# Loads issued part by part, array work ahead of the first norm, value copies on ScalarE, and a new order between two batches of a post-norm transformer block

## The chip, the cores and the metric

The kernel runs on one core of one Trainium2 chip, in one launch. The metric is the device time in microseconds (us). The kernel before took 471.42 us as the median of 3 runs (471.38 to 472.26).

## The reference

For two sequences of 1024 tokens of width 256, in fp32:

```
Xn  = layernorm(X) * ln_g + ln_b
Q, K, V = Xn @ Wq + bq, Xn @ Wk + bk, Xn @ Wv + bv        # 16 heads of 16
A   = softmax(causal(Q K^T / 4));  attn = (A V) @ Wo + bo
x   = layernorm(X + attn)
h   = relu(x @ W1 + b1);  alpha = softmax(h @ W2 + b2)     # 8 maps
y   = layernorm(x + sum_k alpha_k * (x @ V_k^T) @ U_k^T)
```

The rows of A sum to one, so bv can be added to the output of the attention, as `bv @ Wo`, in place of being added to every value.

## The kernel before, in words

Tokens are cut into 8 tiles of 128, and two chunks c of 512; heads into four groups g of four. A list of events, written out in `program_order` (L143 to L213), is walked by every engine; each issues the instructions that it has for an event, in that order, with waits on semaphores between the engines. `attention_order` weaves row maxima, scores and value products of one batch, and `beside` (L183 to L192) hangs further events on its steps; the steps run to 47, so an event at 48 to 50 stands at the end of the batch's attention.

The events that matter here:

- `ln1` (L608), `ln2` (L690), `ln3` (L724): the three norms, on VectorE, four tiles at a time; each is a chain of small instructions.
- `xt` (L762): the normed input is transposed by PE into a bank of PSUM and copied by ScalarE (L517) to `xt`, which lies in the probabilities' buffer `pr[2]`.
- `qk` (L776): PE computes a part of Q or K (m is the half of the heads, w is 0 for Q and 1 for K); ScalarE writes its bf16 high part (L531, semaphore `s_high`), VectorE the rest (L626); `part` then makes the middle part on ScalarE (L536, `s_mid`) and the low part on POOL (L489, `s_low`). The exact fp32 product of a score is rebuilt from six bf16 products.
- `stack` (L420): twelve DMAs, issued by SP, that copy the parts of four heads to the stacks `stq` and `stk`, in two halves of two heads; six of them fill one half.
- `v` (L782): PE computes the values of two tiles in a bank, VectorE adds bv and writes them to `va` (L632). There are four of these in a batch.
- `max` (L790, L646): PE recomputes scores, VectorE takes the row maximum; `split` and `rows` turn the maxima into three rows that are sent to `stq` by DMA; `score` (L812) and `value` (L824) are the attention proper, with the exponentials on ScalarE (L545).
- `ot`, `r1`: the attention's output is transposed and multiplied by Wo; `bo` (L478, POOL) has added bo to the input. `x1t`, `h`, `lg`, `weigh`, `alpha`: the gates. `vx`, `avt`, `u`: the maps.

PSUM is used as two rings. Results for VectorE go to four banks in turn (`n_dve`), those for ScalarE to three (`n_act`); PE may take a bank only when the result that had it before has been read:

```
        n_act = count("xt", "score", "ot", "x1t", "h", "avt")
        n_dve = count("qk", "v", "max", "rows", "turn", "r1", "lg", "vx", "u")
```

SP's queue holds, in the order of the events, the loads of X, of the weights, the stacks, the rows and the stores. Between the batches (b = 0 to 1) the order is

```
            order += ot + first[:parts] + [r4, r6, n] + first[parts:parts + 2] + m[0][9:]
            order += [("load", nb)] + turned + first[parts + 2:parts + 3] + mixed[:parts] + first[parts + 3:]
            order += [("stack", nb, 1, 0)] + mixed[parts:] + second[:parts] + [("alpha", b, 1)] + third[b][:1]
```

where `first` and `second` are xt, qk and stack of the next batch's chunks 0 and 1, `[r4, r6, n]` the last r1 pair and ln2 of this batch, `turned` x1t, `mixed` h, lg and weigh, `m[0][9:]` the last two u, and `third` ln3.

Of the kernel before, what the change touches and what calls it, by code (L numbers as in the profile page):

```python
# [12 lines left out]
P = 128  # L13
# [129 lines left out]
def program_order(batches, groups, tiles, parts):  # L143
# [34 lines left out]
    for b in range(batches):  # L178
# [6 lines left out]
        if nb < batches:  # L185
            beside[30] = [("early", nb)]
            beside[38] = [("ln1", nb, 0, TPC)]
            beside[43] += [("ln1", nb, TPC, TPC)]
        for k, t in zip((13, 17, 21, 25), pairs):
            beside[k] = [("bo", b, t)]  # L190
# [13 lines left out]
        if nb < batches:  # L204
            first, second = begin(nb, 0), begin(nb, 1)
            before = m[1]
            order += ot + first[:parts] + [r4, r6, n] + first[parts:parts + 2] + m[0][9:]
            order += [("load", nb)] + turned + first[parts + 2:parts + 3] + mixed[:parts] + first[parts + 3:]
            order += [("stack", nb, 1, 0)] + mixed[parts:] + second[:parts] + [("alpha", b, 1)] + third[b][:1]
# [6 lines left out]
def block_kernel(nc, x, vecs, rows, wq, wk, wv, wo, w1, w2, vt, ut, out):  # L216
# [16 lines left out]
    with ExitStack() as ctx:  # L233
# [15 lines left out]
        flat = sb("flat", [P, 2 * D + E])  # L249
        ident = sb("ident", [P, P])  # L250
# [48 lines left out]
        s_flat = sem("s_flat")  # L299
        s_w = {n: sem(f"s_w_{n}") for n in ("qk", "v", "o", "1", "2", "vt", "ut")}  # L300
# [33 lines left out]
        n_act = count("xt", "score", "ot", "x1t", "h", "avt")  # L334
        n_dve = count("qk", "v", "max", "rows", "turn", "r1", "lg", "vx", "u")
# [57 lines left out]
        def _(sp):  # L393
# [3 lines left out]
            for ev in order:  # L397
                kind, b = ev[:2]
                if kind == "load":
# [9 lines left out]
                    if b == 0:  # L409
                        sp.dma_start(flat[:], rows.partition_broadcast(P)).then_inc(s_flat, 16)  # L410
                        weight(w_v[:], wv, "v")
                if kind == "early":
# [7 lines left out]
                if kind == "stack":  # L420
                    _, _, g, c = ev

                    sp.wait_ge(s_low, n_part["part", b, KC - 1, c, 1])
# [5 lines left out]
                    for i in range(2):  # L429
# [4 lines left out]
                        row = 0  # L434
                        for part_of_q, parts_of_k in ((0, 3), (1, 2), (2, 1)):
                            rows_ = slice(row, row + parts_of_k * DH)
                            row = rows_.stop
                            same = q_parts[:, part_of_q:part_of_q + 1].to_broadcast([DH, parts_of_k, KC * CHUNK])
                            sp.dma_start(k[rows_, c, heads], k_parts[:, 0:parts_of_k]).then_inc(s_stack[stack_of(b, g)][c][i], 16)
                            sp.dma_start(q[rows_, c, heads], same).then_inc(s_stack[stack_of(b, g)][c][i], 16)  # L440
# [19 lines left out]
        def _(pool):  # L460
# [15 lines left out]
            for ev in order:  # L476
                kind, b = ev[:2]
                if kind == "bo":  # L478
                    pool.wait_ge(s_flat, 16)
# [250 lines left out]
        def _(pe):  # L730
# [29 lines left out]
            for ev in order:  # L760
# [63 lines left out]
                if kind == "value":  # L824
# [8 lines left out]
                    if g == 0:  # L833

                        pe.wait_ge(s_dve_free, n_dve["v", b, kt // 2 * 2])
# [98 lines left out]
```

## Time and profile before

| | |
|---|---|
| median of 3 runs | 471.42 us |
| the profiled execution, its own time | 473.8 us |
| span of the profile | 472.1 us |
| PE busy | 416.1 us, 88% |
| PE weight loads | 208.1 us, 44% |
| VectorE busy | 314.9 us, 67% |
| ScalarE busy | 230.4 us, 49% |
| POOL busy | 73.4 us, 16% |
| mean granted TensorE clock | 0.966 |

The page gives the busy time of each engine over the whole span. The timeline gives instructions in order of time, neighbours of one kind merged: "x16" on a row is a run of 16 of them, and its second number the time from the first's start to the last's end.
### The profile page before, as it was taken

To read this page: it belongs to the slowest core of one execution; us is meant where nothing else is said; L and a number is where in the kernel's file an instruction comes from. 1 tells how busy PE (TensorE), PEld (TensorE's weight loads), DVE (VectorE), ACT (ScalarE), POOL (GpSimd) and SP (SyncE) were. 2 spreads that over 40 slices of the span, in tenths; PEclk is the share of its full clock that TensorE was granted. 3 is DMA by queue.
4 is the path that set the end of the run, shared out by engine and by line. 5 is a ranking of instruction groups with operands and counts; after the bars stand their busy time and mean duration, and the time that the engine had idled before them with its cause. 6 is when DMAs were issued, how large, how long until landed. Compare 5 with 4: busy or idle time off the path is not lost.

```text
span 472.1 us, 7166 instructions
## 1 busy us (share of the span) xinstructions
PE 416.1 (88%) x2512; PEld 208.1 (44%) x2512; DVE 314.9 (67%) x812; ACT 230.4 (49%) x490; POOL 73.4 (16%) x108
## 2 busy tenths in 40 slices
PE   1798897998999989997899989799899999997893
PEld 1355343343344433475447734334334443356452
DVE  5448895898798676244557799689889771225266
ACT  6451554666668475332441155476666846431210
POOL 2042121033120101101120021113222020110000
PEclk9999897999999999998899999899999999999997
DMA  5048883370502000002287028146050000000011
GB/s 179 0 53 101 181 100 41 43 94 3 68 24 69 2 1 0 1 0 91 29 103 115 1 62 104 17 61 77 12 59 3 0 2 0 2 0 0 1 45 44
DMA packets 18147, 21.13 MB, mean 45 GB/s; under 512 B 4672, under 2 KB 11584, under 8 KB 18112
## 3 DMA queue, kind: packets, MB, share of 16 engines
q1 hardware_dynamic: 18061, 20.66, 27.8%
q8 instruction: 20, 0.33, 0.3%
q14 instruction: 15, 0.12, 0.1%
q10 hardware_dynamic: 51, 0.01, 0.0%
HBM read 5.78 MB, written 2.10 MB: 17 GB/s over the span
## 4 chain that ended last, share of the span: by engine, by line
PE 64%; DVE 21%; ACT 6%; DMA 3%; issue 3%; SPq 2%; POOL 0%; DVEq 0%; ACTq 0%
PE ps L756 24%; PE ps L841 13%; PE ps L821 12%; DVE mx L646 11%; PE ps L800 9%; ACT pr L545 2%; DMA stq<-mrow 2%; PE ps L804 2%; PE ps L750 2%; ACT stk L508 2%; DVE st L595 1%; DVE x L602 1%; PE ps L851 1%; PE ps L886 1%; DMA cols<-in_vecs 1%
## 5 line engine op out<-in xcount | busy, mean ns | idle before, releaser
L545 ACT ACTIVATE pr<-ps 128x512 f32<-128x512 f32 (+3 forms) x384 | 167.7, 495 | 129.6 <-PE ps L821 127.9
L646 DVE TENSOR_REDUCE mx<-ps 128x1 f32<-128x512 f32 (+3 forms) x304 | 182.1, 654 | 31.4 <-PE ps L804 23.3
L821 PE MATMUL ps<-stq,stk 99*128 99x512 bf16 (+3 forms) x384 | 119.0, 338 | 13.6 <-DMA stq<-mrow 8.0
L800 PE MATMUL ps<-stk,stq 96*128 96x512 bf16 (+3 forms) x384 | 115.8, 333 | 3.9 <-DVE mx L646 1.4
L498 POOL TENSOR_SCALAR_AFFINE_SELECT pr<-pr 128x512 f32<-128x512 f32 x64 | 40.8, 637 | 274.2 <-ACT pr L545 274.2
L841 PE MATMUL ps<-pr,va 128*32 128x512 f32 (+3 forms) x768 | 82.3, 501 | 0.0
L821 PEld LDWEIGHTS ps<-stq,stk 99*128 99x128 bf16 x384 | 35.1, 99 | 101.0 <-ACT pr L545 53.2
L804 PE MATMUL ps<-mask,ident_b 128*128 128x128 bf16 x256 | 50.3, 223 | 0.0
L800 PEld LDWEIGHTS ps<-stk,stq 96*128 96x128 bf16 x384 | 38.0, 99 | 24.4 <-issue 8.3
L756 PE MATMUL ps<-pr,w_qk 128*128 128x512 f32 x64 | 34.8, 697 | 4.2 <-ACT pr L517 4.2
L756 PE MATMUL ps<-u_t,avt 128*128 128x256 f32 x128 | 30.9, 387 | 2.8 <-ACT avt L567 2.8
L756 PE MATMUL ps<-v_t,x_t 128*128 128x512 f32 x64 | 32.1, 629 | 0.0
L804 PEld LDWEIGHTS ps<-mask,ident_b 128*128 128x128 bf16 x256 | 25.6, 100 | 12.8 <-issue 4.2
L489 POOL TENSOR_TENSOR qk_raw<-res,qk_raw 128x512 bf16<-128x512 f32 x16 | 18.3, 1157 | 70.1 <-ACT qk_raw L536 70.1
L626 DVE SCALAR_TENSOR_TENSOR res<-ps,cols,qk_raw 128x512 f32<-128x512 f32 x16 | 11.9, 750 | 24.7 <-ACT qk_raw L531 20.9
L841 PEld LDWEIGHTS ps<-pr,va 128*32 128x32 f32 x768 | 15.3, 108 | 29.3 <-issue 20.2
L715 DVE TENSOR_TENSOR avx<-ps,alpha 128x512 f32<-128x512 f32 x16 | 11.0, 690 | 23.0 <-PE ps L756 23.0
L756 PEld LDWEIGHTS ps<-u_t,avt 128*128 128x128 f32 x128 | 23.4, 191 | 6.0 <-DVE x L723 3.2
L531 ACT ACTIVATE qk_raw<-ps,cols 128x512 bf16<-128x512 f32 x16 | 11.0, 687 | 29.6 <-PE ps L756 29.6
L756 PEld LDWEIGHTS ps<-pr,w_qk 128*128 128x128 f32 x64 | 14.1, 227 | 21.3 <-issue 20.6
L567 ACT ACTIVATE avt<-ps 128x512 f32<-128x512 f32 x16 | 9.5, 597 | 27.3 <-PE ps L886 27.3
L756 PEld LDWEIGHTS ps<-v_t,x_t 128*128 128x128 f32 x64 | 11.9, 199 | 10.6 <-issue 9.5
(75 smaller groups left out, 338.8 us busy)
## 6 DMA issues: line engine op xcount, KB each, us to landing
stk<-qk_raw SPq DMA_DIRECT2D x32, 96.0 KB, 2.8
stq<-qk_raw SPq DMA_DIRECT2D x32, 96.0 KB, 3.1
x_in<-in_x SPq DMA_DIRECT2D x8, 256.0 KB, 3.3
stk<-qk_raw SPq DMA_DIRECT2D x32, 64.0 KB, 3.2
stq<-qk_raw SPq DMA_DIRECT2D x32, 64.0 KB, 3.2
out_y<-x SPq DMA_DIRECT2D x3, 512.0 KB, 3.0
stk<-qk_raw SPq DMA_DIRECT2D x32, 32.0 KB, 2.9
stq<-qk_raw SPq DMA_DIRECT2D x32, 32.0 KB, 2.5
```

The lines of the kernel that those rows point to most:

```text
L489: pool.tensor_tensor(part(w, c, 2)[:, m], res[:, n_part[ev] % RES], part(w, c, 1)[:, m], ALU.subtract).then_inc(s_low, 1)
L498: pool.affine_select(out=blk, in_=blk, compare_op=ALU.is_ge, fill=0.0, base=0, pattern=[[0, HPG], [1, P]], channel_multiplier=-1).then_inc ...
L531: nc.scalar.activation(part(w, c, 0)[:, m], dve_bank(ev), ACT.Identity, bias=cols[:, 2 + w, m:m + 1]).then_inc(s_high, 1)
L545: nc.scalar.activation(probs(b, g, s)[:, j, q0 - c * CHUNK:], act_bank(ev)[:, q0 - c * CHUNK:], ACT.Exp, scale=DH ** -0.5).then_inc(s_act_ ...
L626: nc.vector.scalar_tensor_tensor(res[:, n_high[ev] % RES], dve_bank(ev), cols[:, 2 + w, m:m + 1], part(w, c, 0)[:, m], ALU.add, ALU.subtra ...
L646: nc.vector.tensor_reduce(dst, src, AX.X, ALU.max).then_inc(s_dve_free, 1)
L715: nc.vector.tensor_tensor(avx[:, t % 2, :].rearrange("p (e r) -> p e r", e=E), dve_bank(ev).rearrange("p (e r) -> p e r", e=E), alpha[:, t ...
L756: last = nc.tensor.matmul(out_, lhs(k), rhs(k), start=(k == 0), stop=(k == n - 1))
L800: last = nc.tensor.matmul(bank[:, i * w:(i + 1) * w], q[0:ROWS, t // TPC, j, tile(t % TPC)], k[0:ROWS, k0 // CHUNK, j, 0:w], start=True, s ...
L804: last = nc.tensor.matmul(bank[:, (i + 1) * w - P:(i + 1) * w], ident_b[:], mask[:], start=False, stop=True)
L821: nc.tensor.matmul(bank[:, q0 - c * CHUNK:], stk[stack_of(b, g)][0:ROWS + PARTS, kt // TPC, j, tile(kt % TPC)], stq[stack_of(b, g)][0:ROWS ...
L841: last = nc.tensor.matmul(values_bank[j * VW:(j + 1) * VW, q0 - c * CHUNK:], va[:, kt, g * HPG + j, :], probs(b, g, s)[:, j, q0 - c * CHUNK:],
```

## The change

The order changes, both in what hangs on the attention's steps and between the batches. A new event `fold` in the first batch computes `bv @ Wo` on PE, with bv as a stationary operand that is repeated over 128 columns, and VectorE adds it to the row of bo that `bo` later adds to the input. The values are then copied from PSUM by ScalarE without a bias, and take a bank of ScalarE's ring. A stack's DMAs wait for the part that they copy, the high parts first, and the pairs are regrouped so that each pair needs one further part. PE runs 20 matmuls of a constant by itself before its first transposes and 5 behind those of the first chunk (`turn_over`); their result is overwritten.

```diff
@@ program_order
+            beside[49] = m[0][7:8] + [("xt", nb, 0, k) for k in ks]
             beside[43] += [("ln1", nb, TPC, TPC)]
+        if b == 0:
+            beside[9] = [("fold", 0)]
...
-            order += ot + first[:parts] + [r4, r6, n] + first[parts:parts + 2] + m[0][9:]
-            order += [("load", nb)] + turned + first[parts + 2:parts + 3] + mixed[:parts] + first[parts + 3:]
-            order += [("stack", nb, 1, 0)] + mixed[parts:] + second[:parts] + [("alpha", b, 1)] + third[b][:1]
+            qk, (here, xt, later) = first[parts:-1], (first[-1:], second[:parts], [("stack", nb, 1, 0)])
+            order += qk[:1] + ot + qk[1:2] + m[0][9:10] + [r4, r6, n] + m[0][10:] + qk[2:3] + [("load", nb)]
+            order += turned + qk[3:] + here + later + third[b][:1] + xt + mixed + [("alpha", b, 1)]
@@ counts
-        n_act = count("xt", "score", "ot", "x1t", "h", "avt")
-        n_dve = count("qk", "v", "max", "rows", "turn", "r1", "lg", "vx", "u")
+        n_act = count("xt", "v", "score", "ot", "x1t", "h", "avt")
+        n_dve = count("qk", "fold", "max", "rows", "turn", "r1", "lg", "vx", "u")
@@ SP, load
                         weight(w_v[:], wv, "v")
+                        for k in range(KC):
+                            sp.dma_start(bv[:, k:k + 1], rows[k * P:(k + 1) * P].rearrange("(p o) -> p o", o=1)).then_inc(s_bv, 16)
@@ SP, stack
-                    sp.wait_ge(s_low, n_part["part", b, KC - 1, c, 1])
...
-                        for part_of_q, parts_of_k in ((0, 3), (1, 2), (2, 1)):
...
+                        made = ((s_high, n_high["qk", b, KC - 1, c, 1]), (s_mid, n_part["part", b, KC - 1, c, 1]),
+                                (s_low, n_part["part", b, KC - 1, c, 1]))
+                        for part_of_q, row, terms in ((0, 0, 3), (1, 3 * DH, 2), (2, 5 * DH, 1)):
+                            sp.wait_ge(*made[part_of_q])
+                            q_rows, k_row = slice(row, row + terms * DH), (5 * DH, 3 * DH, 0)[part_of_q]
+                            k_rows = slice(k_row, k_row + (part_of_q + 1) * DH)
+                            same = q_parts[:, part_of_q:part_of_q + 1].to_broadcast([DH, terms, KC * CHUNK])
+                            sp.dma_start(q[q_rows, c, heads], same).then_inc(s_stack[stack_of(b, g)][c][i], 16)
+                            sp.dma_start(k[k_rows, c, heads], k_parts[:, 0:part_of_q + 1]).then_inc(s_stack[stack_of(b, g)][c][i], 16)
@@ POOL, bo
-                    pool.wait_ge(s_flat, 16)
+                    pool.wait_ge(s_dve_free, n_dve["fold", 0])
@@ ScalarE
+                if kind == "v":
+                    t = ev[2]
+                    act.wait_ge(s_act_full, n_act[ev])
+                    nc.scalar.activation(va[:, t:t + 2, :, 0:DH], act_bank(ev).rearrange("p (t h d) -> p t h d", t=2, h=HEADS),
+                                         ACT.Copy).then_inc(s_act_free, 1)
@@ VectorE (the add of bv in "v" goes)
+                if kind == "fold":
+                    dve.wait_ge(s_flat, 16)
+                    dve.wait_ge(s_dve_full, n_dve[ev])
+                    nc.vector.tensor_tensor(flat[:, D:2 * D], dve_bank(ev)[:, 0:D], flat[:, D:2 * D], ALU.add).then_inc(s_dve_free, 1)
@@ PE
+            def turn_over(n):
+                for _ in range(n):
+                    nc.tensor.matmul(values_bank, ident_b[:], ident_b[:].unsqueeze(1).to_broadcast([P, TPC, P]),
+                                     start=True, stop=True)
+
+            pe.wait_ge(s_mask, 4)
+            turn_over(20)
             pe.wait_ge(s_ident, 2)
...
                     turn(bank, src, k).then_inc(s_act_full, 1)
+                    if ev == ("xt", 0, 0, KC - 1):
+                        turn_over(5)
...
+                if kind == "fold":
+                    bank = take_dve(ev)
+                    weights("o", b)
+                    pe.wait_ge(s_bv, 16 * KC)
+                    product(bank[:, 0:D], lambda k: bv[:, k:k + 1].to_broadcast([P, P]), lambda k: w_o[:, k, :], KC).then_inc(s_dve_full, 1)
                 if kind == "v":
-                    bank = take_dve(ev)
+                    bank = take_act(ev)
...
-                        pe.wait_ge(s_dve_free, n_dve["v", b, kt // 2 * 2])
+                        pe.wait_ge(s_act_free, n_act["v", b, kt // 2 * 2])
```

## Rows read from the trace of the kernel before

**Rows 1.** The page: the chain that ended last, shares of the span by engine.

```profile
PE 64%; DVE 21%; ACT 6%; DMA 3%; issue 3%; SPq 2%; POOL 0%; DVEq 0%; ACTq 0%
```

**Rows 2.** Timeline, first 46 us, PE: start us, us, instruction, [idle before, releaser].

```profile
14.64 9.66 PE L756 MATMUL ps<-pr,w_qk 128*128 128x512 f32 x16 [2.55 <-ACT pr L517]
25.01 3.62 PE L756 MATMUL ps<-w_v,pr 128*128 128x256 f32 x16
28.47 7.03 PE L756 MATMUL ps<-pr,w_qk 128*128 128x512 f32 x16
...
44.96 0.24 PE L810 MATMUL ps<-ident_b,mhl 128*48 128x128 bf16 x1 [0.50 <-DMA stq<-qk_raw]
45.40 0.22 PE L800 MATMUL ps<-stk,stq 96*128 96x128 bf16 x1 [0.20 <-issue]
```

**Rows 3.** Timeline, PE, two bf16 matmuls of 512 columns.

```profile
78.09 1.06 PE L821 MATMUL ps<-stq,stk 99*128 99x512 bf16 x2
```

**Rows 4.** Timeline, first 46 us, ScalarE and VectorE.

```profile
5.72 7.29 ACT L508 ACTIVATE stk<-minus 3x2048 f32<-3x2048 f32 x4
13.04 1.45 ACT L517 ACTIVATE pr<-ps,cols 128x512 f32<-128x512 f32 x2
...
24.34 0.69 ACT L531 ACTIVATE qk_raw<-ps,cols 128x512 bf16<-128x512 f32 x1 [0.51 <-PE ps L756]
...
26.38 1.43 ACT L517 ACTIVATE pr<-ps,cols 128x512 f32<-128x512 f32 x2
...
36.92 3.40 DVE L646 TENSOR_REDUCE mx<-ps 128x2 f32<-128x512 f32 x6
40.66 0.69 DVE L632 TENSOR_TENSOR va<-ps,flat 128x512 f32<-128x512 f32 x1 [0.33 <-PE ps L756]
41.27 2.81 DVE L646 TENSOR_REDUCE mx<-ps 128x2 f32<-128x512 f32 x5
...
44.83 0.68 DVE L632 TENSOR_TENSOR va<-ps,flat 128x512 f32<-128x512 f32 x1
```

**Rows 5.** Timeline, SP's queue: the loads of the first two stacks (24 in all).

```profile
27.93 0.72 SPq L439 DMA_DIRECT2D stk<-qk_raw  x1
...
43.13 0.59 SPq L440 DMA_DIRECT2D stq<-qk_raw  x1
```

**Rows 6.** Timeline between the batches, PE.

```profile
211.73 1.89 PE L756 MATMUL ps<-u_t,avt 128*128 128x256 f32 x8
216.43 2.45 PE L756 MATMUL ps<-u_t,avt 128*128 128x256 f32 x8 [2.81 <-ACT avt L567]
...
232.10 8.44 PE L756 MATMUL ps<-pr,w_qk 128*128 128x512 f32 x12 [1.67 <-ACT pr L517]
240.38 1.88 PE L756 MATMUL ps<-v_t,x_t 128*128 128x512 f32 x4
```

**Rows 7.** Stretches: us, busy time (and count) by engine, then clock, DMA share, GB/s.

```profile
217.90:221.20 3.30, 3.30 (x12) 2.54 (x11) 0.42 (x1) 1.17 (x2) 0.25 (x1) 0.50 0.38 118
...
231.30:238.10 6.80, 6.00 (x7) 2.50 (x8) 5.96 (x26) 1.34 (x2) 0.12 (x1) 0.51 0.70 83
...
240.40:271.10 30.70, 30.70 (x160) 21.57 (x158) 21.38 (x57) 5.75 (x10) 4.32 (x4) 1.00 0.49 70
```

**Rows 8.** Timeline between the batches, VectorE.

```profile
208.85 1.41 DVE L595 BATCH_NORM_STATS2 st<-x_in 128x6 f32<-128x256 f32 x4
...
213.09 1.38 DVE L602 TENSOR_SCALAR x<-x_in,mv,rstd 128x256 f32<-128x256 f32 x4
...
271.38 1.88 DVE L632 TENSOR_TENSOR va<-ps,flat 128x512 f32<-128x512 f32 x3
```

**Rows 9.** Two more stretches, with the columns of rows 7.

```profile
446.20:449.60 3.40, 3.40 (x6) 1.46 (x5) 1.25 (x4) 0.06 (x1) 0.00 (x0) 0.54 0.01 2
...
76.40:79.50 3.10, 3.09 (x10) 1.25 (x10) 1.12 (x2) 1.93 (x4) 0.00 (x0) 0.50 0.02 5
```

**Rows 10.** Groups by form: count | busy us, mean ns | idle before, releaser.

```profile
L756 PE MATMUL ps<-w_o,o_t 128*128 128x256 f32 x64 | 15.1, 383 | 0.8 <-ACT o_t L522 0.8
```

More of the change, by code:

```diff
@@ L249, in block_kernel @@
         flat = sb("flat", [P, 2 * D + E])
+        bv = sb("bv", [P, KC])
         ident = sb("ident", [P, P])
@@ L299, in block_kernel @@
         s_flat = sem("s_flat")
+        s_bv = sem("s_bv")
         s_w = {n: sem(f"s_w_{n}") for n in ("qk", "v", "o", "1", "2", "vt", "ut")}
@@ L433, in _ @@
                         k_parts = parts(1, c)[head].rearrange("p n m s -> p n (m s)")
-                        row = 0
-                        for part_of_q, parts_of_k in ((0, 3), (1, 2), (2, 1)):
[L436 to L440, printed above, removed]
+                        made = ((s_high, n_high["qk", b, KC - 1, c, 1]), (s_mid, n_part["part", b, KC - 1, c, 1]),
[7 more added lines that the diff above has]
+                            sp.dma_start(k[k_rows, c, heads], k_parts[:, 0:part_of_q + 1]).then_inc(s_stack[stack_of(b, g)][c][i], 16)
                     if n == 0 and c == C - 1:
@@ L628, in _ @@
                         part(w, c, 0)[:, m], ALU.add, ALU.subtract).then_inc(s_dve_free, 1)
-                if kind == "v":
-                    t = ev[2]
+                if kind == "fold":
+                    dve.wait_ge(s_flat, 16)
                     dve.wait_ge(s_dve_full, n_dve[ev])
-                    nc.vector.tensor_tensor(
-                        va[:, t:t + 2, :, 0:DH],
-                        dve_bank(ev).rearrange("p (t h d) -> p t h d", t=2, h=HEADS),
-                        flat[:, 0:D].rearrange("p (h d) -> p h d", h=HEADS).unsqueeze(1).to_broadcast([P, 2, HEADS, DH]),
-                        ALU.add).then_inc(s_dve_free, 1)
+                    nc.vector.tensor_tensor(flat[:, D:2 * D], dve_bank(ev)[:, 0:D], flat[:, D:2 * D], ALU.add).then_inc(s_dve_free, 1)
                 if kind == "max":
@@ L788, in _ @@
                         last = product(bank[:, i * D:(i + 1) * D], lambda k: xt[:, c, k, tile(n)], lambda k: w_v[:, k, :], KC)
-                    last.then_inc(s_dve_full, 1)
+                    last.then_inc(s_act_full, 1)
                 if kind == "max":
```

## The prediction

> **What bounds the kernel now.** I read the page first. PE is busy 88% of the span, and 64% of the chain that ended last runs through PE, 21% through VectorE [rows 1]. That says who is late on the whole, not where, so I went to the two places that the change touches. In the timeline of the first 46 us the reader is to see that PE's first products run at half pace, 9.66 us for 16 records where the next 16 of the same kind take 7.03 [rows 2]; the column of the clock still says 1.00 there, since no change of it had been recorded yet, so the durations are what counts. Between the batches, PE's timeline has two holes, 2.81 and 1.67 us [rows 6], and behind each a stretch at clock 0.50 [rows 7]; from 240.4 to 271.1 PE has no idle time, and from 271.1 to 297 it is VectorE that has none (25.56 of 25.90 us) [rows 7]. The attention proper, some 350 us of the span, is hardly touched.
>
> **The start.** ScalarE fills the constant rows until 13.01 and copies the first xt until 14.49, and PE's first product waits for that [rows 2, 4]. So nothing before it can gain. The 20 matmuls cost nothing if they and the first transposes are done by then. Two of this size take 1.06 us at clock 0.50 [rows 3, 9], so 20 take at most 10.6; they start behind POOL's constants, about 2.5 us in, and end by 13.1 at worst, by 7 to 11 more likely, while PE idles 2.55 us before its product. What they can bring is the clock: 9.66 - 7.03 = 2.6 us less for the first 16 records. The bounds are 0 (the clock falls again before 14.64) and 2.6; I take 2.6, since the 5 matmuls behind the transposes leave a hole of only some 2 us, and a hole of 2.81 is followed by full clock for another 1.5 us, until 217.9 [rows 6, 7], which would be covered here at least in part.
>
> The value products now take ScalarE's banks, three in turn, of which the second chunk's xt has two. The second v needs the bank of the first xt, whose copy ends half way through 26.38 + 1.43, at 27.1, where that product started at 25.01 + 3.62 / 2 = 26.8 [rows 2, 4]: +0.3 us on the qk of chunk 1 behind it. VectorE loses its values: the one at 40.66 stands between maxima, but VectorE had waited 0.33 us for it and would now wait for the next maxima's scores, so of 0.69 us some 0.3 counts; the one at 44.83 delays the copy of the rows by 0.2 [rows 4]. ScalarE has no other work there; a copy costs it 0.6 to 0.7 us (half of the 1.45 of two xt copies), hidden, and if that cover were gone, 0.7 us each. Sum: -2.6 + 0.3 - 0.5 = -2.8 us.
>
> The loads part by part. SP issues 24 loads from 27.93 to 43.72 for the first two stacks [rows 5], 0.63 us each, and the first maxima of group 1 at 45.40 need the last of them [rows 2]. The high parts are ready at 25.03 [rows 4], 2.9 us before the low ones; so SP would be 2.6 + 2.9 = 5.5 us earlier, less some 0.3 of short waits. The last load is now 96 KB where it was 32 KB, a few tenths more. But the same maxima wait for PE's rows at 44.96, a chain through qk of chunk 1, the maxima and split, and that chain moves by 2.8 only. Without the earlier issue SP would give 2.6, with it the other chain decides: part by part is worth 0.2 us at the start, and 2.9 if I misread the other chain. I take 0; the 2.8 above stands. For later stacks nothing waits. The rows' DMAs, the weights' loads and the stores are queued behind the stacks on SP, which become free sooner. Two small loads of bv at the start cost SP some 1 us behind the weights, ahead of nothing that is due before 22 us. In the steady part POOL's `bo` waits for the fold instead of for the rows' load, long before its result is needed.
>
> **The fold.** Four records of 256 columns on PE; 64 such of the product with Wo are busy for 15.1 us, 0.24 us each [rows 10]: +0.9 us, if PE is the bound at that step (the chain there runs over PE's value products), +1.8 at the lower clock, 0 if it falls into a wait. I take 0.9. Its add on VectorE is half as wide as an add of values (0.69 us [rows 4]) and, by that, 0.4 us, estimated, in the idle time that VectorE has beside PE's value products.
>
> **Between the batches.** From 213.6 to 240.38, where the maps of the second chunk start, PE loses: 2.81 + 1.67 idle, half of the 3.30 busy us at clock 0.50, half of the 6.00 busy us at 0.51 [rows 6, 7]: 2.8 + 1.7 + 1.65 + 3.0 = 9.1 us. The first hole is there because `u` waits for ScalarE's copy of avt, which stands behind a `part` that waits for VectorE, which is in ln2 from 208.85 to 214.47 [rows 8]. (Times from here on are those of the trace of before, without what the start gives.) In the new order both `part`s and the copy come before ln2, and VectorE does their residues first, so u 2 and u 3 run on. But r1 comes later by two qk products (4 records each, 7.03 / 4 = 1.75 us): r1 ends at 211.5, ln2 runs from 212.4 to 218.0, and x1t waits for it. PE has u 3 (1.8) and one qk (1.75) until 216.8: a hole of 1.2 us. The second hole came from xt copies behind `weigh`; now the xt of chunk 1 stand before h and three qk follow lg at once, and what is left is the wait of lg for h's second copy, 0.7 us as in the last batch. So 9.1 - 1.9 = 7.2 us are to be had from holes and clock. I give one spell of low clock back: in the last batch the same sequence (norm, x1t, h, lg) has 3.4 us at 0.54 behind the logits [rows 9], which is 1.7 us. Together -5.5 us. VectorE has ln3 (5.6 us) now before the softmax: ln3 from 222.3 to 227.9, alpha by 230, avx is due at 233: covered with some 3 us; SP issues the stack's 24 loads from about 221.5 to 237 and the first maxima come at 234 with the first six landed at 228: covered too. From there to 271 PE has no hole [rows 7], so the gain stays.
>
> **The values of the second batch.** Three stand together on VectorE at 271.38, 1.88 us, at the head of the 26 us in which VectorE has no idle time [rows 7, 8]. They go to ScalarE, which is idle there, and their banks no longer hold up the maxima: -1.9 us. The fourth is hidden.
>
> **Sum:** -2.8 + 0.9 - 5.5 - 1.9 = -9.3 us, against 473.8 us of the profiled execution (472.1 of span) 464.5. The median is 2.4 us below that execution, so 462.1 us.
>
> **The rivals.**
> *A, the clock falls back before the first product.* For it: a hole of 1.67 us at 230.4, behind the logits and transposes, was followed by low clock [rows 6, 7], and here are transposes and a hole as well. Against: the 5 matmuls. The start then gives 0.2 us: 462.1 + 2.6 = 464.7 us.
> *B, the gain between the batches goes to VectorE's chain.* The norm is later by 3.5 us and ln3 stands before lg; if ScalarE's queue holds h's copies behind a `part`, alpha comes past 233 and PE waits at avt. With ln2's 3.5 us lost outright, the transition gives 2 in place of 5.5: 465.6 us.
> *C, more than forecast.* No low clock between the batches (-1.7), the fold in a wait (-0.9), part of SP's earlier start counts (-1): 458.5 us.
> *D, slower.* The clock goes low at the hole before x1t and stays low until the maps. Its place is from 216.8 on, where PE has 14 us of work; at half pace they cost 14 more. Then -2.8 + 0.9 - 7.2 - 1.9 + 14 = +3.0: 474.4 us, and it decides from 11 us of low clock's loss on. For it: the order leaves two small holes near each other, and before there were 6.8 us in a row at 0.51. Against: only after a full hole and small matmuls. The Trainium skill, page TensorE: Matmul & The Clock Gate, section A second HAM failure mode: psum-queue depth-cycling, says that short idles between groups of matmuls can throw the clock back again and again; by that rule D is the outcome, 474.4 us. The trace does not bear it out: from 240.4 to 271.1 PE changes between many small groups at 1.00 [rows 7].
> *E, hidden.* The transition is bound by something that I take as covered and the start by SP, so that the sum is within 0.9 us of nothing.
>
> **How the numbers follow.** Forecast 0.47, A 0.18, B 0.12, C 0.14, D 0.04, E 0.05. The forecast's own range, by its bounds (fold 0 to 1.8, clock spell 0 to 3.4, part by part 0 to 2.9), is 459 to 465. The range reaches to A, B and C: 457.5 to 467. Of a change of 0.2% (0.9 us), about what a measurement of this kernel tells from none: faster 0.91 (the first four cases), the same 0.04, slower 0.05 (D and a part of E).
>
> **What would show it.** Right: 16 records of the first qk in about 7.0 us; SP's first stack load at about 22.4, ahead of the low part; the first maxima of group 1 at about 42.6; the first maps of the second chunk on PE at 240.4 - 2.8 + 0.9 - 5.5 = 233.0; no VectorE work on va; the fold's four matmuls at about 83. Wrong: first records again at 0.85 us each (A), a hole at avt 4 behind alpha (B), clock 0.50 from 217 to 233 (D), or maxima of group 1 that wait for a load.

## The result, and the profile after

The changed kernel takes 465.94 us (median of 4 runs, 464.22 to 466.19) against 471.84 for the kernel before: a ratio of 0.9862, 95% interval 0.983 to 0.9895, or 5.9 us. In a second set of runs it was 465.51 us and 0.9869 (0.9834 to 0.9903). The forecast was 462.1 with 457.5 to 467; the sign and the range held, and the gain was 0.6 of what was forecast. The forecast's own range, 459 to 465, did not hold: the result lies in the part that was added for the rivals.

| | before | after |
|---|---|---|
| median | 471.84 us | 465.94 us |
| profiled execution, own time | 473.8 us | 466.19 us |
| its span | 472.1 us | 464.3 us |
| PE busy | 416.1 us | 418.5 us |
| VectorE busy | 314.9 us | 310.2 us |
| ScalarE busy | 230.4 us | 234.3 us |
| mean granted clock | 0.966 | 0.972 |

The page first: the chain is still PE's, with the same share, and VectorE's share is down from 21 to 19%. PE is busy for 2.4 us more than before, though the 25 matmuls of a constant and the fold add 9.5 us to it (7.21, 1.24 and 1.08 in the rows below): the rest of its work took some 7 us less, with less time at low clock. So what left the span is to be looked for in the clock and in the waits, place by place.

```profile
span 464.3 us, 7228 instructions
...
PE 64%; DVE 19%; ACT 7%; SPq 4%; issue 3%; DMA 3%; POOL 1%; DVEq 0%; ACTq 0%
```

**The start**, PE's timeline. The answers to [rows 2] are the rows from 14.53 on.

```profile
2.59 7.21 PE L773 MATMUL ps<-ident_b 128*128 128x512 bf16 x20 [2.59 <-POOL mask L481]
10.12 1.07 PE L760 MATMUL ps<-ident,pr 128*128 128x128 f32 x8 [0.32 <-DVE pr L616]
11.02 1.24 PE L773 MATMUL ps<-ident_b 128*128 128x512 bf16 x5
14.53 8.80 PE L766 MATMUL ps<-pr,w_qk 128*128 128x512 f32 x16 [2.27 <-ACT pr L526]
...
28.06 7.03 PE L766 MATMUL ps<-pr,w_qk 128*128 128x512 f32 x16
```

The 20 matmuls take 7.21 us and end at 9.80, the transposes run at full pace (1.07 us for 8), the 5 matmuls end at 12.26. Then PE waits 2.27 us for ScalarE, and the first 16 records take 8.80 us: neither the 9.66 of before nor the 7.03 of full clock. Here a record is one entry of the trace, two for each fp32 matmul of the program. The first stretch of the next fence says why. Its columns are those of [rows 7].

```profile
14.50:18.30 3.80, 3.77 (x5) 1.63 (x6) 1.00 (x4) 0.39 (x1) 0.00 (x0) 0.56 0.00 0
...
199.00:217.80 18.80, 17.42 (x89) 12.87 (x88) 9.93 (x33) 7.05 (x12) 2.28 (x2) 1.00 0.00 1
217.80:235.10 17.30, 16.09 (x61) 8.61 (x62) 10.57 (x37) 8.86 (x16) 3.66 (x4) 1.00 0.69 134
428.10:434.80 6.70, 5.89 (x13) 3.42 (x14) 0.55 (x2) 1.35 (x3) 0.00 (x0) 0.50 0.00 0
```

For some 3.4 of these 3.8 us the clock was at 0.5: it had been up for the transposes and the 5 matmuls and was lost behind the hole. The other rows are for the parts further down: no low clock from 199 to 235, and 6.7 us of it from 428.

ScalarE's rows show what holds the first product: the fill of constants, and it starts only at 5.62.

```profile
5.62 7.29 ACT L517 ACTIVATE stk<-minus 3x2048 f32<-3x2048 f32 x4
12.94 1.45 ACT L526 ACTIVATE pr<-ps,cols 128x512 f32<-128x512 f32 x2
```

SP's first load, and the end of its queue ahead of the rows of (group 0, chunk 1):

```profile
24.09 0.72 SPq L448 DMA_DIRECT2D stq<-qk_raw  x1
```

```profile
70.83 1.76 SPq L448 DMA_DIRECT2D stq<-qk_raw  x1
72.63 0.59 SPq L449 DMA_DIRECT2D stk<-qk_raw  x1
73.67 0.80 SPq L461 DMA_DIRECT2D stq<-mrow  x1
```

The first load goes out at 24.09, 3.8 us before [rows 5] (5.5 had been forecast, 22.4). But the rows' DMA, ready for issue at 72.9, stands behind two loads, one of which took 1.76 us to issue, and leaves at 73.67, against 74.03 before. This belongs to the execution: in the second trace of the same kernel (changed_again, below) it leaves at 72.80, 0.3 us after VectorE starts the copy that it waits for, and no load is in its way.

**The fold**, on PE, just ahead of a value product:

```profile
81.57 1.08 PE L766 MATMUL ps<-w_o,bv 128*128 128x256 f32 x4
```

**Between the batches**, PE, to be read against [rows 6]:

```profile
211.09 3.62 PE L766 MATMUL ps<-u_t,avt 128*128 128x256 f32 x16
...
217.84 1.06 PE L760 MATMUL ps<-ident,x 128*128 128x128 f32 x8 [1.42 <-DVE x L616]
...
226.37 1.92 PE L766 MATMUL ps<-w,o_t 128*128 128x8 f32 x16 [0.87 <-ACT o_t L529]
...
233.38 1.88 PE L766 MATMUL ps<-v_t,x_t 128*128 128x512 f32 x4
```

The hole before `u` is gone, the one before xt's copies too. One of 1.42 us before x1t and one of 0.87 before the logits are left, and the maps of the second chunk start at 233.38, where they had started at 240.38. In the trace of before, two stretches of low clock, 3.4 and 6.8 us, lie in this part; here there is none.

**The values**: VectorE goes from ln3 to the maxima with nothing between (the 1.88 us of [rows 8] are gone).

```profile
263.09 1.38 DVE L616 TENSOR_SCALAR x<-x,mv,rstd 128x256 f32<-128x256 f32 x4
264.39 2.94 DVE L656 TENSOR_REDUCE mx<-ps 128x1 f32<-128x384 f32 x5
```

**The end**, PE. The hole of 2.69 us before x1t of the last batch is as it was; this time the clock was low behind it for 6.7 us (last row of the fence of stretches), where the kernel before had 3.4 us at 0.54 behind the logits [rows 9].

```profile
421.82 3.62 PE L766 MATMUL ps<-u_t,avt 128*128 128x256 f32 x16
428.13 1.94 PE L760 MATMUL ps<-ident,x 128*128 128x128 f32 x8 [2.69 <-DVE x L616]
430.85 5.62 PE L766 MATMUL ps<-x_t,w 128*128 128x512 f32 x8 [0.78 <-ACT x_t L531]
437.35 1.92 PE L766 MATMUL ps<-w,o_t 128*128 128x8 f32 x16 [0.87 <-ACT o_t L529]
```

### The profile page after: what moved, and what is told of

Its sections match the earlier page's. It is cut to its first block, busy times and chain, and to the rows that moved or that the text cites. A ratio compares the mean times of both kernels' runs of the same rounds, so it can differ in the third digit from the quotient of the medians.

```text
span 464.3 us, 7228 instructions
## 1 busy us (share of the span) xinstructions
PE 418.5 (90%) x2541; PEld 209.1 (45%) x2541; DVE 310.2 (67%) x805; ACT 234.3 (50%) x498; POOL 73.3 (16%) x108
## 4 chain that ended last, share of the span: by engine, by line
PE 64%; DVE 19%; ACT 7%; SPq 4%; issue 3%; DMA 3%; POOL 1%; DVEq 0%; ACTq 0%
PE ps L766 23%; PE ps L868 13%; PE ps L848 12%; DVE mx L656 9%; PE ps L827 9%; PE ps L831 2%; ACT pr L559 2%; DMA stq<-mrow 2%; PE ps L760 2%; SPq L448 2%; SPq L449 2%; ACT stk L517 2%; DVE st L609 2%; DVE x L616 1%; PE ps L878 1%
## 5 line engine op out<-in xcount | busy, mean ns | idle before, releaser
L848 PE MATMUL ps<-stq,stk 99*128 99x512 bf16 (+3 forms) x384 | 118.5, 336 | 13.8 <-DMA stq<-mrow 8.7
L766 PE MATMUL ps<-pr,w_qk 128*128 128x512 f32 x64 | 30.7, 625 | 2.3 <-ACT pr L526 2.3
L766 PE MATMUL ps<-v_t,x_t 128*128 128x512 f32 x64 | 30.4, 600 | 0.0
L766 PEld LDWEIGHTS ps<-pr,w_qk 128*128 128x128 f32 x64 | 12.3, 199 | 15.6 <-issue 15.3
L766 PE MATMUL ps<-x_t,w 128*128 128x512 f32 x32 | 17.2, 671 | 1.8 <-ACT x_t L531 0.8
```

What stands on the lines that cost most here:

```text
L766: last = nc.tensor.matmul(out_, lhs(k), rhs(k), start=(k == 0), stop=(k == n - 1))
L848: nc.tensor.matmul(bank[:, q0 - c * CHUNK:], stk[stack_of(b, g)][0:ROWS + PARTS, kt // TPC, j, tile(kt % TPC)], stq[stack_of(b, g)][0:ROWS ...
```

## The experiments

Twelve runs, each timed in five rounds beside the kernel before on the same chip (6 or 12 executions of each). The ratio in each is to the kernel before. Since one execution differs from the next by 2 to 5 us, I read every trace by the same five marks, from which a part's worth can be told without its neighbours' luck. Each line is one execution. The luck of the clock inside a part stays in it: a stretch of 3.4 us at half pace costs up to 1.7 us. fill_early has no line, for the reason given there.

```
marks (us): a first qk on PE; b first score of (group 0, chunk 1), batch 0; c first product
with Wo, batch 0; d first maps of chunk 1, batch 0; e first product with Wo, batch 1; end
               a       a-b     b-c     c-d     d-e     e-end   span
before         14.64   61.77   79.28   84.69   137.45  94.27   472.1
changed        14.53   61.50   79.56   77.79   135.88  95.04   464.3
changed_again  15.29   59.91   79.59   77.79   136.55  94.97   464.1
old_order      14.62   59.26   80.10   81.63   135.55  95.04   466.2
no_warm        13.81   61.01   80.71   77.79   136.68  95.10   465.1
loads_whole    15.67   58.56   79.61   77.79   136.59  95.08   463.3
v_on_dve       14.08   58.38   78.67   81.17   137.53  94.17   464.0
warm_14        14.17   58.27   80.78   77.78   136.75  95.05   462.8
fold_moved     14.40   59.40   78.64   79.49   135.91  94.86   462.7
order_only     15.75   60.72   78.58   79.47   138.91  95.27   468.7
fill_fold      12.46   58.40   77.14   79.49   136.48  94.93   458.9
holes          12.55   58.52   77.15   79.41   134.43  95.54   457.6
holes_lg       12.45   58.66   77.16   77.73   135.87  92.13   454.0
```

**old_order.** The two edits of the order taken back:

```diff
-            beside[49] = m[0][7:8] + [("xt", nb, 0, k) for k in ks]
...
-            order += qk[:1] + ot + qk[1:2] + m[0][9:10] + [r4, r6, n] + m[0][10:] + qk[2:3] + [("load", nb)]
+            order += ot + first[:parts] + [r4, r6, n] + first[parts:parts + 2] + m[0][9:]
...
```

> The changed kernel with the order between the batches as it was (and the next batch's first xt not hung on step 49); all else of the change stays. Theory: the order alone carries the gain between the batches. In the two traces the first maps of the second chunk start 7.0 us earlier with it, and of the whole 7.6 us between the profiled executions it is nearly all. So this kernel is 6.5 to 7.5 us slower than the changed one, about 472 to 473 us, equal to the kernel before within 1 us (it keeps 1.8 us of the values, gives 0.9 for the fold). Rival: the gain is the clock's luck, and the holes matter less; then it is slower by 3 us or less, and PE's holes of about 2.8 and 1.7 us come back without the two stretches at clock 0.50.

Measured: 470.23 us, ratio 0.9958 (0.9924 to 0.9992): about 4.5 us slower than the changed kernel by the ratios. From c to d it takes 81.63 us against 77.79, with 3.4 us of low clock (at 215) where the trace of the kernel before had 10.2. So the order is the largest part of the change, as the theory has it, but its size lies between the two: against this execution of the old order it is worth 3.8 us of this part, and against the one of the kernel before 6.9.

**order_only.** The kernel before with just those edits.

> The kernel before with the new order between the batches (and the next batch's first xt on step 49), nothing else of the change. Theory: from the first product with Wo of batch 0 (155.7 us) to the first maps of its second chunk takes 77.8 us if the clock holds and 79.5 or 81.2 with one or two windows' worth of low clock, against 84.7 in the kernel before; so 4 to 7 us faster than before, about 466 to 467 us. Rival: the order needs the values off VectorE's ring to work; then less than 4 us.

Measured: 470.31 us, ratio 0.9974 (0.9947 to 1.0001). From c to d 79.47 us, as the theory says (84.69 before); but the whole is 1.2 us faster, give or take 1.3, and the rival's "less than 4" is right in its number. Of the 5.2 us of this part, 1.5 are given back from d to e and 1.0 behind e. PE waits for VectorE at 266 (1.00 us) and 271 (1.43 us), and in this execution the clock fell there, for about 3.4 us. The kernel before has the same two waits (0.99 and 1.43 us, at 272 and 277), and the clock stayed up:

```profile
264.00:271.00 7.00, 4.98 (x24) 1.77 (x22) 6.86 (x15) 4.16 (x8) 1.27 (x2) 1.00 0.22 75
271.00:274.60 3.60, 2.98 (x14) 0.85 (x15) 2.60 (x8) 0.39 (x1) 0.00 (x0) 0.62 0.02 5
```

That the order needs the values off VectorE, the rival's reason, is not shown: v_on_dve (next) has the new order with the values on VectorE, its clock stays up at 271, and d to e is 137.53, as before. The small worth has a plainer reading in part: this profile is 3.4 us shorter than that of the kernel before, and the latter is some 2 us above its own median, with 10.2 us of low clock from c to d. Why the order is worth 4.5 us when it is taken out and 1.2 when it is put in alone stays open.

**v_on_dve.** Values with their bias on VectorE, no fold: the edits of `v` and `fold` taken back on every engine.

```diff
-                    bank = take_act(ev)
+                    bank = take_dve(ev)
...
-        if b == 0:
-            beside[9] = [("fold", 0)]
```

> The changed kernel with the values added to their bias on VectorE in its ring, as before, and without the fold. Theory: +1.8 us ahead of the second batch's maxima, +0.5 in the first batch, -0.9 for the fold that is left out: 1.2 to 1.6 us slower. Rival: with the new order VectorE is no longer the bound at 264 us, so the values are hidden and the missing fold makes it 0.5 to 0.9 us faster.

Measured: 468.04 us, ratio 0.9921 (0.9887 to 0.9954), 2.8 us slower than the changed kernel by the ratios; 1.2 to 1.6 had been expected, and the intervals allow it. The mechanism is in the rows: three values, 1.88 us, stand ahead of the maxima again. From d to the long row of 22 maxima VectorE takes 38.96 us (232.30 to 271.26), 38.95 in the kernel before, 37.07 in the changed one (233.38 to 270.45).

```profile
263.31 1.88 DVE L639 TENSOR_TENSOR va<-ps,flat 128x512 f32<-128x512 f32 x3
```

**no_warm.** Both calls of `turn_over` deleted.

> The changed kernel without the 25 matmuls of a constant. Theory: they speed up only the first 16 records of qk, 8.80 us in the changed kernel and 9.66 before, since the clock is lost again in the hole of 2.27 us; so qk of chunk 0 takes 9.6 to 9.7 us and the kernel is 0.6 to 1.0 us slower. Rival: SP's queue of 24 loads ahead of the rows of (group 0, chunk 1) sets the pace at 56 to 74 us and hides it; then no difference, and the rows' DMA is issued at the same time as in the changed kernel (73.7 us, within 0.3).

Measured: 467.5 us, ratio 0.9932 (0.9903 to 0.996), some 3 us slower than the changed kernel, more than the 0.6 to 1.0 of the theory; the intervals touch only with that of the changed kernel's second set. The records behave as the theory says:

```profile
10.09 1.94 PE L760 MATMUL ps<-ident,pr 128*128 128x128 f32 x8 [10.09 <-DVE pr L616]
13.81 9.78 PE L766 MATMUL ps<-pr,w_qk 128*128 128x512 f32 x16 [1.78 <-ACT pr L526]
```

9.78 us for the 16 records, against 8.80, 8.57 or 7.1 with the matmuls in front. The rival is wrong: the rows' DMA leaves at 72.39 and not at 73.7, so SP's queue does not fix that time. But this profile does not show where 3 us go. It reaches b at 74.82, 1.2 us before the changed kernel's first trace (a is 0.7 us earlier, and no load delays the rows), and has lost all but 0.1 of that by c, with 6.8 us of low clock where the changed kernel had 3.4. That the 25 matmuls are worth 3 us stands on the times alone; the rows show 1.0 of it, on the first records.

**changed_again** and **warm_14.** The changed kernel once more, and with

```diff
-                        turn_over(5)
+                        turn_over(14)
```

> The changed kernel once more, unaltered, beside the others of this call: the yardstick for effects of one or two us. Expected: ratio to the kernel before 0.983 to 0.990, as in its first runs. Its profile also tells whether the first 16 records of qk take 8.8 us again or 7.1, as they do in three of the four kernels just run with the same 25 matmuls in front: theory, this is not the kernel's but the execution's, since the array's clock is lost in the hole of some 2.3 us in some executions and not in others.

> The changed kernel with 14 in place of 5 matmuls behind the transposes, which fill PE's hole before the first qk. Theory: the clock is never lost there, the 16 records take 7.1 us in every execution, and the time is 0 to 1.7 us lower in the median and its highest runs come down. Rival: what is gained at 23 us is hidden by SP's queue before 74 us; then the same time, with the rows' DMA of (group 0, chunk 1) at the same place behind a busy queue.

Measured: 465.51 us, ratio 0.9869 (0.9834 to 0.9903), and 464.81 us, ratio 0.9867 (0.983 to 0.9904). With the hole filled the 16 records take 7.03 us and a to b 58.27 us, the shortest of all, in this one profile; the changed kernel has 8.57 us and 59.91 in its second. In the total the two can't be told apart. With the same 25 matmuls in front, old_order, loads_whole, v_on_dve and fold_moved have 7.10 or 7.11 us, and the changed kernel twice has 8.6 to 8.8. The length of the hole does not sort them: the clock was lost behind 2.27 and 3.01 us and held over 1.81, 1.96, 2.28 and 3.35. That the loss belongs to the execution and not to the kernel is likely, since PE runs the same up to there, but no kernel was seen with both outcomes at this hole. Elsewhere one was: the changed kernel's first trace has 3.4 us at 0.50 from 49.1, its second has none there.

**loads_whole.**

```diff
                     _, _, g, c = ev
+                    sp.wait_ge(s_low, n_part["part", b, KC - 1, c, 1])
                     n = b * G + g
```

> The changed kernel, but every stack waits for the last low part before its first load, as before; order and sizes of the loads stay. Theory: the loads start at about 26.1 us in place of 24.1, the 24th is issued at about 42.5 and lands near 45, where the maxima of group 1 start at 44.5 in the changed kernel: 0.3 to 0.8 us slower. Between the batches nothing waits for a load. Rival (my first sum misjudged the loads): the early parts carry more, 2 us or more slower, with PE waiting for a load at the first maxima of chunk 0 or behind 235 us.

Measured: 465.02 us, ratio 0.985 (0.9824 to 0.9877): not slower at all. The rows show the theory's few tenths, an idle time of 0.47 us of PE ahead of the first maxima of group 1, which the view puts down to no engine (that it is the load is my reading):

```profile
43.73 0.24 PE L838 MATMUL ps<-ident_b,mhl 128*48 128x128 bf16 x1 [0.65 <-DVE mhl L673]
...
44.44 0.22 PE L828 MATMUL ps<-stk,stq 96*128 96x128 bf16 x1 [0.47 <-issue]
```

A wait of this size can't be seen in the total. The rival is excluded: waiting for the high parts only is worth nothing that can be measured in this kernel. The new order of the loads and their new sizes stayed in; no run takes them back alone.

**fold_moved.**

```diff
-            beside[9] = [("fold", 0)]
...
+            at_rows = rest.index(("rows", 0, 0, 1))
+            rest[at_rows + 1:at_rows + 1] = [("fold", 0)]
```

> The changed kernel with the fold right behind the rows of (group 0, chunk 1), where PE waits 3.5 us for their DMA, in place of step 9. Theory: at step 9 PE has no idle time and the fold costs its whole 1.0 us (the lead over the kernel before fell from 1.0 to 0.13 us over it); in the wait it costs nothing: 0.9 us faster, and the first value product behind the wait is at the same distance from it. Rival: it was hidden at step 9 and the lead was lost to other things: the same time.

Measured: 464.4 us, ratio 0.9849 (0.9809 to 0.9889). The total can't tell 0.9 us from nothing; the marks can: b to c takes 78.64 us, against 79.56 and 79.59 in the changed kernel with a stretch of low clock of the same length at the same place (3.4 us, about 1 us behind b). In the wait the fold costs nothing:

```profile
69.52 1.13 PE L767 MATMUL ps<-w_o,bv 128*128 128x256 f32 x4 [0.36 <-DVE mx L657]
70.48 0.22 PE L849 MATMUL ps<-stq,stk 99*128 99x128 bf16 x1
...
73.80 0.39 PE L849 MATMUL ps<-stq,stk 99*128 99x512 bf16 x1 [2.30 <-DMA stq<-mrow]
```

In this execution the clock was low behind the logits (mean 0.72 from 224 to 230), and c to d took 79.49.

**fill_early.** ScalarE's fill no longer stands behind the wait for the load of cols.

```diff
-            act.wait_ge(s_cols, 16)
-
-            nc.scalar.activation(le[:, 0, 0, 0:1], cols[:, 0, 0:1], ACT.Exp)
             act.wait_ge(s_one_minus, 1)
...
                                      ACT.Copy).then_inc(s_minus, 1)
+            act.wait_ge(s_cols, 16)
+            nc.scalar.activation(le[:, 0, 0, 0:1], cols[:, 0, 0:1], ACT.Exp)
```

> The changed kernel with ScalarE's fill of the constant rows (4 instructions, 7.3 us) ahead of its wait for the load of cols instead of behind it. In all traces so far this fill, not the norm and not PE, ends just before the first xt copies, and its start moves by 1.9 us between executions with the landing of that load. Theory: the first qk starts at about 12.3 us instead of 13.8 to 15.7 and with no hole in which the clock can be lost, and the whole kernel is 2 to 3.5 us faster than the changed one. Rival: SP's queue of loads is the bound of the first 74 us, then 1 us or less.

Measured: 462.09 us, ratio 0.9801 (0.9767 to 0.9834), 3.2 us under changed_again by the ratios. Its profiled execution had a mean granted clock of 0.557 and took 684.74 us; it is in no comparison, and the rows are read from the next kernel.

**fill_fold.** Both of the last two edits.

> The changed kernel with ScalarE's fill ahead of its wait for cols and with the fold in PE's wait for the rows of (group 0, chunk 1). Theory: the two gains add, about 3 and 0.9 us under the changed kernel: 461 to 462 us, the first qk at about 12.3 us with its 16 records in 7.1. Rival: SP's 24 loads ahead of the rows of (group 0, chunk 1) take the gain; then that DMA is issued right behind the last load and the kernel is no faster than with the early fill alone (462.1).

Measured: 461.47 us, ratio 0.9782 (0.9741 to 0.9822). ScalarE and PE at the start:

```profile
2.09 7.29 ACT L515 ACTIVATE stk<-minus 3x2048 f32<-3x2048 f32 x4
9.41 0.20 ACT L519 ACTIVATE le<-cols 128x1 f32<-128x1 f32 x1
10.87 1.45 ACT L526 ACTIVATE pr<-ps,cols 128x512 f32<-128x512 f32 x2 [1.25 <-PE ps L760]
```

```profile
11.10 1.24 PE L773 MATMUL ps<-ident_b 128*128 128x512 bf16 x5
12.46 7.11 PE L766 MATMUL ps<-pr,w_qk 128*128 128x512 f32 x16
```

The fill runs from 2.09 to 9.38 and is off the path; the first qk starts at 12.46 right behind the 5 matmuls, with no hole, and takes 7.11 us. b is reached at 70.86, 5.2 us ahead of the changed kernel's first trace and 4.3 ahead of its second. The rival is wrong: the rows' DMA leaves at 68.46, behind VectorE's copy and 0.6 us after the last load was issued.

**holes** and **holes_lg.** On top of fill_fold, matmuls of the constant ahead of four of PE's waits (six in holes_lg), written to the bank that its next result overwrites. The last two lines of the diff, ahead of the logits, are in holes_lg alone:

```diff
+                    if kind == "x1t" and c == C - 1 and k == 0:
+                        turn_over((5, 9)[b], bank)
...
+                        if g == 0 and c == 1:
+                            turn_over((6, 8)[b], bank)
                         pe.wait_ge(s_rows[c], 16 * (b * G + g + 1))
...
+                    if c == C - 1:
+                        turn_over(4, bank)
```

> As fill_fold, and PE runs matmuls of a constant in the bank that its next result will overwrite, where it waits: 6 and 8 of them ahead of the first score of (group 0, chunk 1) in the two batches (waits of 3.5 and 2.7 us), 5 and 9 ahead of x1t of chunk 1 (1.4 and 2.7 us). Theory: the stretches of low clock at 76, 288 and 428 us follow those holes; with the holes filled they go, each 1.7 to 3.3 us: 3 to 7 us less than fill_fold. Rival: the clock does not look at the last hole, or the matmuls outlast it and delay the work: within 1 us of fill_fold.

> As holes, with 4 more such matmuls ahead of the logits of chunk 1 of each batch (a hole of 0.87 us, then 16 matmuls of 8 columns). Theory: behind the logits the clock fell in the kernel before (231 and 446 us); in the executions where it still would, 1.7 us less, in the others nothing or 0.1 us more. Rival: it costs up to 0.9 us a batch, since the logits are late and nothing was lost.

Measured: 458.43 us, ratio 0.972 (0.9679 to 0.9761), and 454.57 us, ratio 0.9642 (0.9606 to 0.9678). The first is 3 us under fill_fold, as expected at its lower end. The second is 3.9 us lower still, where 1.7 us had been expected for a stretch behind the logits. The theory took the holes one by one. In the traces, filling one hole let the loss move to the next: in fill_fold the clock falls at 422, behind the hole before x1t, for 6.8 us; in holes, with that hole filled, it falls at 428.7, behind the logits, as long; in holes_lg it falls behind neither. The stretch of holes, then three of fill_fold, then the same three of holes_lg:

```profile
428.70:435.50 6.80, 6.80 (x12) 3.22 (x12) 1.82 (x7) 0.23 (x1) 0.00 (x0) 0.50 0.00 1
```

```profile
282.00:290.00 8.00, 5.28 (x29) 2.16 (x26) 3.00 (x7) 3.08 (x6) 0.96 (x2) 0.57 0.08 12
418.00:424.00 6.00, 3.31 (x16) 2.73 (x16) 4.87 (x24) 0.05 (x1) 0.00 (x0) 0.87 0.00 0
424.00:432.00 8.00, 6.35 (x13) 2.64 (x11) 0.00 (x0) 2.52 (x4) 0.00 (x0) 0.67 0.01 2
```

```profile
282.00:290.00 8.00, 7.13 (x51) 2.88 (x48) 4.96 (x10) 4.59 (x9) 0.94 (x2) 1.00 0.01 2
418.00:424.00 6.00, 4.51 (x22) 2.29 (x20) 3.02 (x12) 1.09 (x2) 0.00 (x0) 1.00 0.00 0
424.00:432.00 8.00, 8.00 (x34) 4.39 (x33) 1.82 (x7) 1.60 (x3) 0.00 (x0) 1.00 0.00 0
```

And PE in the last batch of holes_lg. The matmuls fill 2 of the 2.7 us before x1t and all of the wait before the logits; only then does the clock stay up through the tail (e to end 92.13 us, 94 to 95.5 in every other kernel).

```profile
417.88 2.11 PE L773 MATMUL ps<-ident_b 128*128 128x512 bf16 x9
420.65 1.09 PE L760 MATMUL ps<-ident,x 128*128 128x128 f32 x8 [0.66 <-DVE x L616]
422.57 3.67 PE L766 MATMUL ps<-x_t,w 128*128 128x512 f32 x8 [0.83 <-ACT x_t L531]
426.08 1.03 PE L773 MATMUL ps<-ident_b 128*128 128x512 bf16 x4
427.02 1.95 PE L766 MATMUL ps<-w,o_t 128*128 128x8 f32 x16
```

What they cost is small: b is reached 0.2 us later than in fill_fold, and c to d takes 77.73 us with no low clock in it, as in the changed kernel's clean executions (77.79), so the 5 and 4 matmuls between the batches cost nothing there. The logits of batch 0 start at 218.99 us, in holes at 218.94, and the 1.7 us by which holes is longer from c to d (79.41) are its 3.4 us of low clock behind those logits.

```profile
205.00:228.00 23.00, 22.44 (x89) 12.26 (x88) 15.64 (x62) 9.83 (x17) 3.94 (x4) 1.00 0.53 102
```

```profile
226.00 1.88 PE L766 MATMUL ps<-v_t,x_t 128*128 128x512 f32 x4
```

One stretch of low clock is left before the end, 3.4 us at 261.7; d to e is 135.87, 1.4 us longer than in holes, which has none in that part. By the marks holes_lg gains 1.7 us from c to d and 3.4 behind e and gives back 1.4 between. It is the fastest version of this study, 10 to 11 us under the changed kernel.

**The parts together.** Taken out of the changed kernel one at a time, the order is worth 4.5 us, the values with the fold 2.8, the 25 matmuls about 3 and the early loads nothing. That is some 10 us where the whole change gives 5.9. Each of these has an interval of about 2 us to either side, and each trace has its own stretches of low clock; whether the parts overlap or the noise makes up the difference, the runs do not tell.

## Why the prediction was right or wrong

**The main steps held, by rows.** Between the batches the working gave 7.2 us from holes and clock; c to d shrank by 6.9 (84.69 to 77.79). The hole before x1t was put at 1.2 us and was 1.42, the wait of the logits at 0.7 and was 0.87, ln3 was put from 222.3 to 227.9 and ran from 222.05 to 227.84. The stretch of low clock of 1.7 us that I gave back did not occur in the changed kernel's profiles and did in fold_moved and fill_fold (79.49, which is 77.79 + 1.7): against this profile of before, c to d gives -5.2 with it, near the -5.5 of the sum, and -6.9 without. The values gave 1.9, as forecast (38.95 to 37.07). The fold cost 0.95 (fold_moved), forecast 0.9. The loads part by part gave nothing, as taken. Of the rivals, B (VectorE's chain takes over) is excluded by c to d, E (hidden) by the total, and D (low clock through the transition) did not occur. C's first part, no low clock between the batches, did occur; its second, the fold in a wait, did not, and the kernel was slower than forecast. The Trainium skill, page TensorE: Matmul & The Clock Gate, section A second HAM failure mode: psum-queue depth-cycling, has short idles between groups of matmuls as a cause of lost clock. The traces bear it out more than I had thought: the clock fell somewhere behind idle times of 0.87 to 3.5 us in every trace, and holes_lg gained by filling such holes.

**The start was mis-sized.** The term was -2.8 and, in the profiled execution, a and a to b together gave -0.4. Two things took it. The clock was lost in the hole before the first product, which was rival A at 0.18; its price was right only in part, since the 16 records gained 0.9 and not 0. And the rows' DMA stood behind SP's loads, for 0.8 us, in this execution and not in the second. Where the clock held at the first product with the same 25 matmuls or more in front, a to b is 58.3 to 59.4 (58.27 warm_14, 58.38 v_on_dve, 58.56 loads_whole, 59.26 old_order, 59.40 fold_moved), 2.4 to 3.5 us less than before; up to 1.7 of that is another stretch of low clock, at 50 us, which the kernel before, the changed kernel's first trace and fold_moved have and the others lack. What I missed lies ahead of the term: the first product hangs on ScalarE's fill, and that on the landing of one load, which moved a between 13.8 and 15.8 us from one trace to the next. fill_early and fill_fold show it: with the fill off that load, the kernel is 3.2 us faster and a is 12.5.

**The other step that failed is the last one**, "The median is 2.4 us below that execution, so 462.1 us". It took the offset of one profiled execution of one kernel as a constant. That execution (473.8 us, clock 0.966) was one of the longer ones; the profiled one of the changed kernel (466.19) is 0.25 us above its own median. Part of what differs is how long the clock was low: of 57 further executions of the kernel before, eight at a mean clock of 0.976 have spans of 467.8 to 469.3, and the two at 0.958 have 474.9 and 475.8. It is not all: at 0.972 alone they go from 467.7 to 470.7. So the loss of clock in that one execution was partly counted twice, once in the 4.65 us of low clock that were to be had between the batches and once in the 2.4. Of the 3.8 us between 462.1 and 465.94, the offset is 2.4 - 0.25 = 2.15. The other 1.7 lie between the 464.5 of the sum and the 466.19 of the profiled execution, by the marks: the start +2.4, b to c -0.6 (forecast +0.9, the fold; marks +0.28), c to d -1.4, d to e +0.3 (forecast -1.9; marks -1.57), e to the end +0.8, and 0.2 from what lies around the span. The start's error is thus the largest, and two gains beyond the forecast (c to d, b to c) hid 2.0 us of it and of the offset. That the result still lies in the range is in part luck: the forecast's own range left out the value 0 for the first 16 records, which the working had as a bound, and only the rivals' part, up to 467, covered it.

**What was not seen ahead** is the end. I had left it out of the sum, and in its instructions nothing changed; but the changed kernel had 6.7 us of low clock there where the kernel before had 3.4. Where the clock falls in the last batch is no property of the hole alone: the hole of 2.69 us before x1t has 6.8 us of low clock behind it in nine traces and none in two, before and v_on_dve, where 3.4 us lie behind the logits instead (e to the end 94.2 and 94.3 us in these two, 94.9 to 95.3 in the nine). What decides it was not found.

## What to carry to other kernels

Where TensorE is the bound, count the us at low clock beside the idle us: here each hole of 1 to 3 us risked 3.4 or 6.8 us at half pace behind it, and matmuls of a constant, put into the waits, were worth 6.9 us (fill_fold to holes_lg), more than the reordering (4.5 us at most); filling some of the holes moved the loss to the next one. Before forecasting from one profiled execution, look at the clock and span of several: an offset between profile and median is part of the luck of that execution. And put work that waits for no load (here a fill of constants) ahead of the first wait of its queue: it was 3 us here, with no other change.

## What the runs showed of the hardware that I had not expected

- Between the first products and the end of PE's work, low clock comes in stretches of 3.4 or 6.8 us in every trace (fill_early's apart). It differs between two executions of one kernel: the changed kernel's have 3.4 us from 49.1 in the one and none there in the other, 3.4 at 291 and 6.8 at 288.
- Behind the hole ahead of the first qk, 1.8 to 3.4 us long, it came in two traces of the six with the same 25 matmuls in front, at 2.27 and 3.01 us and not at 3.35.
- One execution of fill_early ran at a mean granted clock of 0.557 over its span of 683 us, and one of the kernel before at 0.745 over 540.9 us.
- Single DMA issues on SP that usually take 0.59 us took 1.0 to 1.8 us, about once or twice in 24 (70.83 in the changed kernel).
